# Expert tiles that fetch their transposed halves, in an attention and mixture-of-experts kernel

## The reference, cut to what matters

```python
scores = jnp.einsum('bsqd,bskd->bsqk', qh, kh) / math.sqrt(hd)   # hd = 16, 16 x 16 per token
scores = jnp.where(mask, scores, NEG_INF)
out = jnp.einsum('bsqk,bskd->bsqd', softmax(scores), vh)
...
x = x + xattn(_layernorm(x), ctx_1024, ctx_1024)
...
logits = xf @ gate_w.T + gate_b            # xf = _layernorm(x), 8 experts
top1 = jnp.argmax(logits, axis=-1)
for e in range(8):
    h = jax.nn.relu(xf @ w1[e].T + b1[e])  # 256 -> 1024
    y = h @ w2[e].T + b2[e]                # 1024 -> 256
    out = out + jnp.where((top1 == e)[:, None], y, 0)
x = x + out
```

## Time and profile before

| | |
|---|---|
| median of three runs | 480.92 us (479.22 to 481.33) |
| span of the profiled execution | 492.6 us |
| PE busy in it | 402.1 us (82%) |
| DVE busy | 346.3 us (70%) |
| ACT busy | 177.5 us (36%) |
| POOL busy | 208.7 us (42%) |
| mean granted PE clock | 0.962 |

### The profile page before, as it was taken

The page is one execution under the profiler, slowest core; times in us unless marked ns, Lnnn a source line. Parts: engine busy times, 40 slices in busy tenths (PEclk is TensorE's granted clock), DMA queues, the critical chain, the costliest instruction groups (busy, mean ns, idle before and its releaser), DMA issues.

```text
span 492.6 us, 16316 instructions
## 1 busy us (share of the span) xinstructions
PE 402.1 (82%) x5967; PEld 338.3 (69%) x5967; DVE 346.3 (70%) x777; ACT 177.5 (36%) x317; POOL 208.7 (42%) x213
## 2 busy tenths in 40 slices
PE   0135868888888866897999999779999999999992
PEld 0025757887787765896887877557778877877871
DVE  7978969789945863477757877457666666766662
ACT  3343255542624221342434433224333333433420
POOL 8345374334673467523723242642333323233221
PEclk9999999999999999975699999889999999999998
DMA  8999578899685664377612232544333322222210
GB/s 282 414 305 218 135 170 241 212 259 260 160 220 119 152 167 107 106 173 181 207 45 67 68 76 81 185 131 155 90 68 77 77 62 62 69 60 61 84 31 0
DMA packets 105162, 69.39 MB, mean 141 GB/s; under 512 B 78077, under 2 KB 88190, under 8 KB 104576
## 3 DMA queue, kind: packets, MB, share of 16 engines
q1 hardware_dynamic: 75696, 56.67, 41.9%
q10 hardware_dynamic: 25984, 3.21, 4.6%
q0 software_dynamic: 3408, 8.46, 4.6%
HBM read 48.28 MB, written 12.57 MB: 124 GB/s over the span
## 4 chain that ended last, share of the span: by engine, by line
PE 55%; DMA 11%; SPq 9%; DVE 9%; issue 6%; POOL 5%; ACT 2%; ACTq 1%; another core or an unknown queue 1%; POOLq 0%; DVEq 0%
PE s_ps L1229 20%; SPq L305 8%; PE at_ps L1245 6%; DMA arena<-qv_hl 6%; PE pv_ps L1245 6%; PE pv_ps L1143 6%; PE s_ps L1111 3%; PE lg_ps L1171 3%; PE pv_ps L1246 3%; PE at_ps L1246 3%; POOL qv_hl L987 2%; PE tr_ps L1156 2%; DMA arena<-x 2%; PE st_ps L1196 2%; POOL k_hl L995 1%
## 5 line engine op out<-in xcount | busy, mean ns | idle before, releaser
L1229 PEld LDWEIGHTS s_ps<-arena 128*128 x1872 | 132.7, 99 | 52.2 <-issue 14.6
L1229 PE MATMUL s_ps<-arena 128*128 128x128 f16 x1872 | 158.6, 222 | 8.4 <-DVE arena L906 5.1
L915 DVE SCALAR_TENSOR_TENSOR arena<-arena,s_ps 128x512 f32<-128x512 f32 x78 | 53.6, 687 | 48.6 <-PE s_ps L1229 35.9
L1076 POOL DMA_INDIRECT result<-arena x39 | 38.8, 995 | 95.5 <-DVE arena L940 91.6
L1111 PEld LDWEIGHTS s_ps<-k_hl,arena 128*128 128x128 f16 x1536 | 54.3, 118 | 29.9 <-DMA arena<-qv_hl 22.1
L1111 PE MATMUL s_ps<-k_hl,arena 128*128 128x16 f16 x1536 | 54.7, 179 | 23.3 <-DMA arena<-qv_hl 19.3
L1143 PE MATMUL pv_ps<-a_hl,arena 128*128 128x16 f16 x1536 | 54.7, 179 | 19.7 <-DMA arena<-qv_hl 15.9
L1143 PEld LDWEIGHTS pv_ps<-a_hl,arena 128*128 128x128 f16 x1536 | 53.5, 118 | 22.8 <-DMA arena<-qv_hl 18.3
L1245 PE MATMUL at_ps<-arena,k_in 128*128 x160 | 60.9, 383 | 0.8 <-DVE k_hl L926 0.6
L1245 PE MATMUL pv_ps<-arena,x_in 128*128 x152 | 58.1, 383 | 0.1
L1069 POOL TENSOR_TENSOR arena<-arena 128x256 f32<-128x256 f32 x39 | 30.7, 786 | 60.7 <-DMA arena<-b 60.6
(11 more groups left out here) (143 smaller groups left out, 614.2 us busy)
## 6 DMA issues: line engine op xcount, KB each, us to landing
arena<-w SPq DMA_DIRECT2D x28, 512.0 KB, 6.1
arena<-sorted_rows SPq DMA_DIRECT2D x39, 130.0 KB, 2.4
arena<-b SPq DMA_DIRECT2D x39, 128.0 KB
arena<-qv_hl SPq DMA_DIRECT2D x70, 64.0 KB, 3.5
k_in<-k_t SPq DMA_DIRECT2D x16, 256.0 KB, 3.9
v_in<-v_t SPq DMA_DIRECT2D x16, 256.0 KB
arena<-x SPq DMA_DIRECT2D x4, 1024.0 KB, 12.1
o_sb<-x_r SPq DMA_DIRECT2D x16, 256.0 KB, 3.8
```

The costliest lines, as they stand in the source:

```text
L915: eng.scalar_tensor_tensor(out=h_in[:, c].rearrange("p (k t) -> p k t", t=P), in0=bias, scalar=W_SCALE, in1=h_ps[c][:].rearrange("p (k t) ...
L1076: eng.indirect_dma_start(out=out, out_offset=bass.IndirectOffsetOnAxis(ap=rows[:, r, :].bitcast(I32)[:, D + 2:D + 3], axis=0), in_=rows[:, ...
L1229: k = eng.matmul(o, weights_of(j, w + k_ * H + n * P, P), xt[:, j % 2, k_ * P:(k_ + 1) * P], start=k_ == 0 and w is HI_1 and xt is xt_hi, ...
```

## The change

Rows are normalised once per group before the scatter, no longer once per tile after the fetch. ACT writes the normalised rows of half a group into `xn1` (four activations of 128x256) and rounds them to f16 (`x1_hi`, one copy of 128x1024), POOL makes `x1_lo`. Both halves travel in the scattered row, which grows from 260 to 516 values (1040 to 2064 bytes). A tile's fetch is now two transfers on SP: a transposing one of the 512 f16 values into `xt` (three buffers, `XB`), and one of the 260 values as before. PE's two transposes, ACT's `xn2` and `xt_hi` and DVE's `xt_lo` are gone. The due times of every step are now a table `TIMES`; `weave` sorts by it. The descriptor scratch of the software queue is cut to 4096 bytes, since `pay` and `xn1` need room. The filler transfers grow with the row, to 1032 values per partition.

```diff
-    ROW = D + 4
+    FETCHED = D + 4
+    ROW = FETCHED + D
...
+        xn1 = sb("xn1", [P, G // 2, D])
+        x1_hi, x1_lo = [pay[:, :, FETCHED:].bitcast(F16)[:, :, n * D:(n + 1) * D] for n in range(2)]
...
-        FR = 6
+        FR, XB = 6, 3
...
-                    eng.dma_start(rows[:, r, :], sorted_rows[bass.ds(row, P), :]).then_inc(s_rows[r], 16)
-                    yield tile_at(j) - 2.6
+                    if j >= XB:
+                        sp.wait_ge(s_up, 2 * (j - XB + 1))
+                    eng.dma_start_transpose(xt[:, j % XB], sorted_halves[bass.ds(row, P), 2 * FETCHED:]
+                                            ).then_inc(s_xt[j % XB], 16)
+                    eng.dma_start(rows[:, r, :], sorted_rows[bass.ds(row, P), 0:FETCHED]).then_inc(s_rows[r], 16)
+                    yield
...
-            def expert_inputs():
-                for j in range(NTILES):
-                    r = j % FR
-                    yield tile_at(j)
-                    act.wait_ge(s_rows[r], 16 * (j // FR + 1))
-                    act.wait_ge(s_xt2, j)
-                    eng.activation(xn2, rows[:, r, 0:D], ACT.Identity, scale=rows[:, r, D + 1:D + 2],
-                                   bias=rows[:, r, D:D + 1]).then_inc(s_xn2, 1)
-                    yield tile_at(j) + 1.5
-                    act.wait_ge(s_xt2, j + 1)
-                    act.wait_ge(s_up, 2 * (j - 1))
-                    eng.copy(xt_hi[:, j % 2], xt2_ps).then_inc(s_xt_hi, 1)
+            def normalised_rows():
+                for g in range(NG):
+                    for m in range(2):
+                        half = slice(m * G // 2, (m + 1) * G // 2)
+                        for b in range(half.start, half.stop):
+                            yield
+                            act.wait_ge(s_ln1, g + 1)
+                            act.wait_ge(s_x1_lo, 2 * g + m)
+                            eng.activation(xn1[:, b - half.start], pay[:, b, 0:D], ACT.Identity, scale=pay[:, b, D + 1:D + 2],
+                                           bias=pay[:, b, D:D + 1]).then_inc(s_xn1, 1)
+                        yield
+                        act.wait_ge(s_xn1, G * g + half.stop)
+                        eng.copy(x1_hi[:, half], xn1[:]).then_inc(s_x1_hi, 1)
...
-            def expert_inputs():
-                for j in range(NTILES):
-                    yield tile_at(j) + 2.0
-                    dve.wait_ge(s_xt_hi, j + 1)
-                    dve.wait_ge(s_up, 2 * (j - 1))
-                    eng.tensor_tensor(xt_lo[:, j % 2], xt2_ps, xt_hi[:, j % 2], ALU.subtract).then_inc(s_xt_lo, 1)
...
+            def low_rows():
+                for g in range(NG):
+                    for m in range(2):
+                        half = slice(m * G // 2, (m + 1) * G // 2)
+                        yield
+                        pool.wait_ge(s_x1_hi, 2 * g + m + 1)
+                        eng.tensor_tensor(x1_lo[:, half], xn1[:], x1_hi[:, half], ALU.subtract).then_inc(s_x1_lo, 1)
...
+                        pool.wait_ge(s_x1_lo, 2 * g + 2)
                         eng.indirect_dma_start(
...
-            def expert_inputs():
-                for j in range(NTILES):
-                    yield tile_at(j) + 0.6
-                    pe.wait_ge(s_q, NC)
-                    pe.wait_ge(s_xn2, j + 1)
-                    pe.wait_ge(s_xt_lo, j)
-                    for k_ in range(KD):
-                        k = eng.transpose(xt2_ps[:, k_ * P:(k_ + 1) * P], xn2[:, k_ * P:(k_ + 1) * P], ident[:])
-                    k.then_inc(s_xt2, 1)
...
-                            pe.wait_ge(s_xt_lo, j + 1)
-                            pe.wait_ge(s_xt_hi, j + 1)
+                            pe.wait_ge(s_xt[j % XB], 16 * (j // XB + 1))
...
-    nc = bacc.Bacc("TRN2", target_bir_lowering=False, num_devices=1)
+    nc = bacc.Bacc("TRN2", target_bir_lowering=False, num_devices=1, dynamic_dma_scratch_size=4096)
```

More of the change, by code:

```diff
@@ L38, in wait_ge, with weave @@
             self.passed[sem] = value
-def weave(*lanes):
-    due = [(next(lane, None), n) for n, lane in enumerate(lanes)]
-    due = [d for d in due if d[0] is not None]
-    while due:
-        turn = min(due)
-        due.remove(turn)
-        again = next(lanes[turn[1]], None)
-        if again is not None:
-            due.append((again, turn[1]))
+def weave(times, **lanes):
+    turns = sorted((t, n, k) for n, name in enumerate(lanes) for k, t in enumerate(times[name]))
+    lane = list(lanes.values())
+    for steps in lane:
+        next(steps)
+    for _, n, _ in turns:
+        next(lane[n], None)
+    assert all(next(steps, True) for steps in lane)
 def xattn_moe_kernel(nc, x, x_t, x_r, k_t, v_t, gate_w, gate_b, w1, b1, w2, b2, out):
@@ L210, in xattn_moe_kernel @@
         s_rows = [sem(f"s_rows{n}") for n in range(FR)]
+        s_xt = [sem(f"s_xt{n}") for n in range(XB)]
         s_b1, s_b2 = [[sem(f"{w}_{n}") for n in range(2)] for w in ("s_b1", "s_b2")]
@@ L244, in xattn_moe_kernel @@
         LATER = 3
-        TILE = 5.7
+        TILE = 5.3
         UNIT = TILE / KH
@@ L425, in fill @@
                     for m in range(1 if n < E - 1 else 1 + SPARE // (2 * P)):
-                        yield fill_at(next(at))
+                        yield
                         if n + m == 0:
@@ L942, in results @@
                             op0=ALU.mult, op1=ALU.add).then_inc(s_y, 1)
-            weave(constants(), statistics(), spreads(), queries(), softmax(), outputs(), layer_norms(), choose(), counts(), plans(),
-                  weights(), expert_inputs(), hiddens(), rests(), results())
+            weave(TIMES["DVE"], constants=constants(), statistics=statistics(), spreads=spreads(),
+                  queries=queries(), softmax=softmax(), outputs=outputs(), layer_norms=layer_norms(),
+                  choose=choose(), counts=counts(), plans=plans(), weights=weights(), hiddens=hiddens(),
+                  rests=rests(), results=results())
         @block.gpsimd
```

400 lines of the change are left out of this document (235 added, 165 removed), and 98 rows, old and new, of tables (TIMES, act, op1).

## The result

The changed kernel is 3.9% slower: 499.35 us median (498.44 to 501.54, 4 runs) against 480.07 (477.74 to 481.33, 4 runs), ratio 1.0386 (1.032 to 1.0452). I had forecast 468. One thing is needed to read the numbers. The kernels ran in sets, each on one chip and together with runs of the kernel before. It is not simply the chip: on chip 5 the kernel before took 478.36 us in one set and 501.06 in another, seven minutes later. The cause is open. So a kernel is compared by its ratio to runs of the kernel before in its own set, and traces of the same set are set side by side where there are any.

A forecast was written before the change was run, and what follows sets the result against it. PE was taken to bound the expert stage, and the length of each chunk's round to count in attention. Savings of 9.0 and 4.0 us, other terms 0, gave 480.9 - 13.0 = 468 us, range 454 to 493.

The forecast's parts named there:

- The base: Whole kernel: the profiled 492.6 us is 11.7 above the median 480.92, carried over unchanged, part of it PE's clock.
- Steady tiles, -9.0: Expert tiles: PE loses two f32 transposes per tile, 39 x 0.23 = 9.0 us saved.
- Transposing transfers, 0: Tile fetches on SP: each transposing transfer lands in about 3 us, issued early enough to cost 0.
- The third rival: Expert tiles: transposing transfers set the pace at 7.0 us per tile, 67 us more, 535 us; chance 0.08.
- Added per group, 0: Mostly attention: added ACT and POOL pieces fit into idle time and cost 0, bounds 0 and 16 us.
- The fourth rival: Attention: its round gets longer, all 16 us of POOL's pieces showing, 484 us; chance 0.06.
- The opening, -4.0: Before the last chunk's outputs: up and down units moved ahead fill PE's idle time, 4.0 us saved.
- PE's idle time in 230 to 250 us: Sign at the opening: PE would be idle under 1 us in this stretch.
- The fillers, 0: Before tile 11's fetch: twelve transfers take 30 us, 14 us lost, the same as the 13.9 lost now.
- the gap of 25 us: Sign before tile 11's up matmuls: a gap over 25 us would make the forecast wrong.
- the second rival: Tile 11: the twelve fillers hold it, deciding from 43 us of filler time; 495 us, at worst 515; chance 0.10.

The follow-up runs named there:

- e_afterorder: The kernel before in the changed kernel's order, with none of its other work and one wait added; 509.91 us, 1.0651.
- c_before: The kernel before, unchanged, traced again in the set of 495, one of the slower kind; 495.87 us.
- e_placed2: The changed kernel in before's order, added pieces placed behind softmax weights, group 3's counts and fillers earlier; 491.71 us, 0.9851 in the set of 500.
- c_before2: The kernel before, unchanged, traced again in the set of 500, beside the changed kernel.
- e_latepart: The changed kernel with e_placed2's order up to the last chunk's softmax and its own order from there; 496.00 us, 1.0335.
- c_placed2: e_placed2 once more, unchanged, in the set of 478; 490.58 us, 1.0244 of the kernel before.
- e_earlypart: The changed kernel with its own order up to the last chunk's softmax and e_placed2's order from there; 502.80 us, 1.0472.
- the repairs: The changed kernel with rank matmuls of groups 0 and 1 later and chunk 15's spread, outputs and sum earlier; together 497.86 us, 1.0421.
- e_beforeorder: The changed kernel with its shared steps put back into before's order on every engine, only new steps placed anew; 504.80 us, 1.0532.

## Why the prediction was wrong

**The base.** I laid part of the 11.7 us between trace and median to PE's clock. In the set of 495 the kernel before took 495.19 us with a mean granted clock of 0.909 and 495.19 with 0.989, and the changed kernel took 498.85 with 0.989 and 498.44 with 0.845. The clock is not it: the trace is one of the slower kind.

**Steady tiles, -9.0: right, and too small.** From tile 17 to 38 the changed kernel takes 110.9 us, 5.28 a tile; e_afterorder in a like set 117.3, 5.59. Over 39 tiles 11.9 us. The transposes account for 0.23 of the 0.31. The rest may be the short irregular delays of the old path (steps of up to 6.5 us in c_before), of which none is left, as PE is busy 126.00 of 126 us; I made no test of that.

**Transposing transfers, 0: right.** They land in 3.0 us in the steady part, at a DMA share of 0.48, and PE does not wait for one there. The third rival falls. The Trainium skill, "VectorE: DVE Perf Modes", "The three transpose paths", gives 1309 ns for a block of 128x128 by DMA, by which four blocks one after another are an estimated 5.2 us. The trace does not agree: the transfer of 128 rows by 512 values lands in 3.0. SyncE's issue of one takes 1.23 us in the median, which I had not priced.

**Added per group, 0: wrong.** This is the first step that failed. In the best order tried, the pieces and the wider rows still put the last outputs 11.0 us later (e_placed2 against c_before2), 3.3 of it by chunk 7. I had bounded it by 0 and 16 and taken 0 because POOL idles 30.6 us ahead of such pieces. That idle time is part of the chunk's round: POOL waits in it for ScalarE, and a piece of 2.14 us that stands ahead of the softmax weights delays the round. And I looked only at engines, not at `pay`, which the low halves keep back from the scatters and the scatters (landing in 5.4 us, 3.8 in e_afterorder) from the next group's copies. The fourth rival had this mechanism, at 0.06. What share each of the two has is not shown.

**The opening, -4.0: wrong sign.** The first up matmul does stand ahead of the last outputs, and tile 0 gains by it, 3.9 us in e_latepart against c_placed2. But the last outputs come 16.2 us later there, with them group 3, and at tile 2 it is 4.8 us behind. PE's idle time in 230 to 250 us was 3.2 us, not under 1. I read how much work was moved ahead and not what it waits for: the first ups waited 6.16 us with no cause shown; low weight halves came at 255.0 us just ahead of them.

**The order of attention: not priced at all.** This is the second step that failed. The new order changed every engine's turns, and I weighed it at the places that I had looked at, none of them in attention. It costs 8.7 us at the last outputs (e_earlypart against c_placed2), 6.2 of them ahead of the first outputs, and 12.2 us at the end there. That an order alone can cost so much, e_afterorder shows.

**The fillers, 0: the place right, the reason incomplete.** I took 30 us and PE work of 15.8 to cover it. They took 33.5, for 26.1 of which SyncE had not yet issued the fetch, and tile 11 came 12.5 us after tile 10, 7.2 over the pace, well under the gap of 25 us by which I would have been wrong. (The trace counts a filler at 516.0 KB where the earlier trace rows have 260.0; my 528 mixed units.) What I missed is that the first filler hangs on the counts of group 3, and with it all that SyncE does behind it. It is the second rival's mechanism, and in the sets of 478 to 480 it makes a floor under tile 11, so that the repairs ahead of it did not pay. Tiles 6 and 7, which took 8.7 and 7.2 us, are not its work. Their fetches were out before the first filler, and PE waited in tile 6 for VectorE's routing of group 3:

```profile
305.01 0.19 PE L1346 MATMUL lg_ps<-onehot,before 128*128 128x64 bf16 x1 [1.20 <-DVE seen L963]
```

In e_afterorder, with none of the change's work, the two take 8.3 and 7.3 us.

The sum: my terms gave -13.0, and the median rose by 19.3. In the sets of 478 to 480 the best order tried is 12.2 us above the kernel before, and the changed kernel another 8.8 above that. The 8.8 are the order's. Where the 12.2 lie is open, as no trace shows the kernel before at 478 us. In the set of 500, against c_before2, the order has 25.8 of the 36.8 us at the last outputs and all of the loss at tile 38, where e_placed2 is 4.2 us ahead.

Between the traces of the kernel before of the earlier trace rows and the changed kernel, the last outputs are 33.1 us later. By c_placed2 as the step between, some 10 are the changed work, 8.7 attention's order, and the other 14 the handover. The floor at tile 11 takes part of it back: tile 17 is 17.2 us later than in the first trace (360.9), tile 38 8.9. These differences are between unlike sets; the median's 19.3 us is not.

## What to carry over

When a change rewrites the order of the work, price the order by itself: the old work in the new order is one run, and here it showed 6.5%. For each added step ask what buffer it keeps and who waits for that buffer, and not only whether its engine has idle time; idle time inside a round is not free. Move a step on every engine that it crosses, and look for the next floor (here counts, fillers, tile 11) before counting on a gain ahead of it.

## What the runs showed of the hardware

VectorE's subtraction took three times as long beside GpSimd's. In e_beforeorder's timeline the same operation takes 0.68 us with no subtraction on GpSimd and 2.19 with GpSimd's piece running:

```profile
317.99 0.68 DVE L1049 SCALAR_TENSOR_TENSOR k_hl<-arena,k_in 128x512 f16<-128x512 f32 x1
320.82 2.12 POOL L1158 TENSOR_TENSOR pay<-xn,pay 128x1024 f16<-128x1024 f32 x1 [2.09 <-ACT pay L718]
321.30 2.19 DVE L1049 SCALAR_TENSOR_TENSOR k_hl<-arena,k_in 128x512 f16<-128x512 f32 x1 [1.24 <-ACT k_in L727]
```

With GpSimd idle, 70 operations of this form took 0.68 us in the median; the three beside a piece of this size took 2.05 to 2.19. The one shown ended 0.55 us after GpSimd's piece (323.49 and 322.94), so it may have been held rather than slowed; the trace does not tell. Either way an added piece on GpSimd can cost VectorE 1.5 us more, and hold the tile that waits for it.

Attention did not follow PE's clock. In 90 to 240 us it was granted 0.55 in c_placed2 and 1.00 in e_placed2, and the same kernel's last outputs began at 244.5 and 246.0 us:

```profile
90.00:240.00 150.00, 114.47 (x2224) 106.19 (x2223) 110.78 (x222) 66.90 (x114) 79.16 (x67) 0.55 0.72 179
```

```profile
90.00:240.00 150.00, 116.54 (x2229) 107.69 (x2229) 109.62 (x221) 66.81 (x114) 78.37 (x65) 1.00 0.71 180
```

A chunk's 96 matmuls of 16 columns took 3.32 us at the lower level (244.47 us, c_placed2) and 3.38 at the higher (111.72 us, e_placed2).

And the sets differ by kernel: e_placed2 took 490.6 and 491.7 us in sets in which the kernel before took 478.4 and 500.3. A ratio from one set does not hold for another.
